# A graph and recurrent kernel: edge places computed in six parts beside the scatter, and four unread TensorE products in every recurrent step

## The reference, cut to what matters

```python
x_proj = jnp.einsum('btd,gd->btg', x, W_ih) + b_ih + b_hh
def step(carry, xp):
    h, c = carry
    gates = xp + h @ W_hh.T                      # 256 -> 1024
    i, f, g, o = jnp.split(gates, 4, axis=-1)
    c = jax.nn.sigmoid(f) * c + jax.nn.sigmoid(i) * jnp.tanh(g)
    h = jax.nn.sigmoid(o) * jnp.tanh(c)
    return ((h, c), h)
```

## Time and profile before

| | us |
|---|---|
| three executions | 31170.26, 31184.28, 31179.84; median 31179.84 |
| profiled execution, its own time | 31181.4 |
| its span, first to last instruction | 31179.7 |
| PE busy | 26082.7 (84% of the span) |
| PE weight loads | 21913.3 (70%) |
| DVE busy | 11210.6 (36%) |
| ACT busy | 8537.5 (27%) |
| POOL busy | 7747.7 (25%) |
| mean granted TensorE clock | 0.631 of full |

### The profile page before, as it was taken

One profiled execution on the slowest core, in us unless ns is written; L12 is line 12 of the kernel. 1 busy time (PEld: TensorE's weight loads), 2 busy tenths in 40 slices (PEclk: granted clock), 3 DMA queues, 4 the chain that ended last, 5 costly groups with the idle time before them and its releaser, 6 DMA issues. The chain is left out here.

```text
span 31179.7 us, 1124934 instructions
## 1 busy us (share of the span) xinstructions
PE 26082.7 (84%) x456492; PEld 21913.3 (70%) x456597; DVE 11210.6 (36%) x40897; ACT 8537.5 (27%) x40793; POOL 7747.7 (25%) x12838
## 2 busy tenths in 40 slices
PE   0002556788777799999999999999999999999998
PEld 0002334333665688888888888888888888888887
DVE  7002333777555333333333333333333333333334
ACT  0000001688111132222222222232222222222322
POOL 1776771677776000000000000000000000000000
PEclk9998778999888655555555555555555555555555
DMA  0002331000333000000000000000000000000000
GB/s 36 1 1 71 104 105 24 7 2 2 97 99 93 33 1 1 1 1 1 1 1 1 1 1 1 1 1 1 1 1 1 1 1 1 1 1 1 1 1 9
DMA packets 370440, 557.74 MB, mean 18 GB/s; under 512 B 177610, under 2 KB 254830, under 8 KB 369006
## 3 DMA queue, kind: packets, MB, share of 16 engines
q0 software_dynamic: 263728, 458.62, 5.9%
q1 hardware_dynamic: 106686, 98.81, 1.0%
HBM read 496.64 MB, written 60.32 MB: 18 GB/s over the span
## 5 line engine op out<-in xcount | busy, mean ns | idle before, releaser
L1160 PE MATMUL banks<-ls_xp,ls_sel 128*128 128x64 f32 x37500 | 9641.6, 430 | 18.2 <-DVE ls_w L1223 18.2
L1160 PEld LDWEIGHTS banks<-ls_xp,ls_sel 128*128 128x128 f32 x37500 | 8466.7, 325 | 1376.1 <-issue 1376.1
L1173 PE MATMUL banks<-ls_w,ls_ht 128*2 128x64 f32 x200000 | 6735.4, 311 | 0.0
L1147 POOL TENSOR_TENSOR ls_d<-ls_tf,ls_cell 128x2 f32<-128x2 f32 x6250 | 1241.9, 199 | 19305.7 <-ACT ls_tf L1188 19305.7
L1173 PEld LDWEIGHTS banks<-ls_w,ls_ht 128*2 128x2 f32 x200000 | 5585.4, 127 | 0.0
L1229 DVE STREAM_TRANSPOSE ls_f_cols<-banks 128x64 f32<-128x64 f32 x6250 | 1561.5, 250 | 7590.1 <-PE banks L1167 7590.1
L1178 PE MATMUL banks<-ls_w,ls_ht 128*2 128x64 f32 x100000 | 4068.7, 311 | 0.0
L436 PE MATMUL banks<-ag_rows,ag_pick 128*128 128x256 f32 x3328 | 1204.8, 526 | 3392.9 <-DMA ag_rows<-y_table,ag_idx 3359.0
L1167 PE MATMUL banks<-ls_w,ls_ht 128*1 128x64 f32 x100000 | 3777.1, 299 | 0.0
L1188 ACT ACTIVATE ls_tf<-ls_f_cols 128x2 f32<-128x2 f32 x6250 | 1286.8, 206 | 8783.7 <-DVE ls_f_cols L1229 8776.7
L436 PEld LDWEIGHTS banks<-ag_rows,ag_pick 128*128 128x128 f32 x3328 | 831.5, 262 | 3765.6 <-DMA ag_rows<-y_table,ag_idx 2759.9
(11 more groups left out here) (256 smaller groups left out, 19365.3 us busy)
## 6 DMA issues: line engine op xcount, KB each, us to landing
ag_rows<-y_table,ag_idx POOLq DMA_INDIRECT x1664, 2.7
mx_rows<-alpha_dst_table,mx_idx POOLq DMA_INDIRECT x1664, 2.3
at_rows<-wh_table,at_idx POOLq DMA_INDIRECT x1664, 2.8
projections<-xp_out SPq DMA_DIRECT2D x7, 3584.0 KB, 10.4
rec_table<-st_rec,st_idx POOLq DMA_INDIRECT x1563, 2.1
ls_xp<-projections SPq DMA_DIRECT2D x1250, 20.0 KB
rec_table<-zero POOLq DMA_DIRECT2D x5, 2496.0 KB, 20.9
rec_part<-rec_table SPq DMA_DIRECT2D x5, 2496.0 KB, 19.9
```

The lines of the kernel that those rows point to most:

```text
L1160: x = nc.tensor.matmul(bank[:, 0:HD], sel[:, u, :], xp[:, b, lo:lo + HD], start=True, stop=False)
L1173: m = nc.tensor.matmul(banks_ig[s][32 * j:32 * j + 2, 0:HD], ht[:, v, c, 1 - r:3 - r], w[:, c, j, lo:lo + HD], start=False, stop=(r, c) == ...
```

## The change: what it does, and the diff

`stage_normalise` keeps only its constants, and `stage_places` becomes empty except for the number of parts, 6. All that they did stands in `stage_scatter`, in one block of the program, so that the engines are no longer held by a barrier between them. DVE counts all edges as before; it makes `REC` after the count and not ahead of it. Then it gives places in six parts of 260 columns (the last has 263), each with its own loop over the 49 blocks. One more small copy per block carries the running offset from part to part. ACT begins to stage records as soon as part 0 has its places (`placed`), and POOL's indirect DMAs follow. Behind part 5 DVE makes `BW` in a loop of its own, and then the layer norm of x, whose square root is one instruction for all blocks, which ACT does after part 3's records. x is loaded and y stored by SP in the same block. POOL clears the record tables before its first indirect DMA, as before.

```diff
+            for c in range(PARTS):
+                act.wait_ge(placed, c + 1)
+                if c == 0:
+                    stage_half(0, 0)
+                    stage_half(0, 1)
+                with act.Fori(0, IT - (c == 0)) as t:
+                    restage(t, c * IT + (c == 0))
+                if c == ROOT_AT:
+                    act.wait_ge(normed, 2 * NB + 1)
+                    nc.scalar.sqrt(root[:, :], ve[:, :]).then_inc(rooted, 1)
...
+            def place(c, a, w):
+                base = c * NB * 4
+                with dve.Fori(0, NB) as b:
+                    vec.tensor_single_scalar(in_b[:, 0:w], hi[:, a:a + w], item[:, ds(b, 1)], ALU.is_equal).then_inc(s_item, 1)
+                    dve.wait_ge(s_item, b * 4 + (base + 1))
+                    vec.tensor_tensor_scan(rank[:, 0:w], in_b[:, 0:w], in_b[:, 0:w], off[:, ds(b, 1)], ALU.add, ALU.bypass).then_inc(s_item, 1)
+                    dve.wait_ge(s_item, b * 4 + (base + 2))
+                    own_wait(dve, g)
+                    vec.tensor_copy(off[:, ds(b, 1)], rank[:, w - 1:w]).then_inc(s_item, 1)
+                    vec.copy_predicated(pos[:, 0:w], in_b[:, 0:w], rank[:, 0:w]).then_inc(s_item, 1)
+                    dve.wait_ge(s_item, b * 4 + (base + 4))
...
+            for c in range(PARTS):
+                place(c, c * W, W if c < PARTS - 1 else W + REST)
```

```diff
+    wake = sb("ls_wake", [P, 512], BF16)
...
                     if u == LU - 1:
                         x.then_inc(xp_used, 1)
+                    for j in range(4):
+                        nc.tensor.matmul(g["ps"][6][32 * j:32 * j + 1, :], wake[:, 0:1], wake[:, :], start=True, stop=True, tile_position=(0, 32 * j))
                     pe.wait_ge(h_ready, i * PER + (k + 1))
...
-                    nc.gpsimd.tensor_tensor(d1[:, 2:2 * SC:SC], tf[:, :], c_now, ALU.mult).then_inc(f_mul, 1)
+                    nc.gpsimd.tensor_tensor(d1[:, 2:2 * SC:SC], tf[:, :], c_now, ALU.mult).then_inc(scan_in, 1)
...
+            vec.memset(wake[:, :], 1.0)
...
-                    dve.wait_ge(f_mul, i * PER + (k + 1))
-                    dve.wait_ge(ig_act, i * PER + (k + 1))
+                    dve.wait_ge(scan_in, i * (2 * PER) + (2 * k + 2))
```

More of the change, by code:

```diff
@@ L136, in stage_normalise @@
 def stage_normalise(nc, sb, sem, g):
-    t = norm_tiles(sb, sem, "ln0")
-    yt = sb("ln0_out", [P, GB, D])
-    x_loaded, pads, step, stored, made = sem("x_loaded"), g["started"], t["step"], sem("y_stored"), sem("consts_made")
+    made = sem("consts_made")
     with nc.Block() as block:
[L141 to L149, removed]
         @block.gpsimd
@@ L159, in _, with stage_scatter @@
             pool.wait_ge(made, 3)
[L161 to L174, removed]
-def stage_places(nc, sb, sem, g):
[L179 to L189, removed]
+def stage_places(nc, sb, sem, g):
+    g["parts"] = 6
+def stage_scatter(nc, sb, sem, g):
+    SH = SU // 2
+    per = SU // WAYS
+    FULL = EC // SU
+    REST = EC - FULL * SU
+    PARTS = g["parts"]
+    IT = FULL // PARTS
+    W = IT * SU
+    ROOT_AT = 3
+    src = sb("src_i", [P, EC], I32)
+    hi_i = sb("hi_i", [P, EC], I32)
+    hi = sb("hi", [P, EC])
+    dst = sb("dst_i", [P, EC], I32)
+    ew = sb("ew_in", [P, EC])
+    in_all = sb("in_all", [P, EC])
+    in_b = sb("in_b", [P, W + REST], I32)
+    rank = sb("rank", [P, W + REST])
+    pos = sb("pos", [P, W + REST])
+    pos_i = sb("pos_i", [P, W + REST], I32)
+    col_i = sb("col_i", [P, W + REST], I32)
     upper = sb("upper", [P, P])
     ones = sb("ones_c", [P, P])
-    cnt = sb("cnt", [EP, NB])
+    cnt = sb("cnt", [P, NB])
     tot = sb("tot", [P, NB])
@@ L339, in _, with stage_half, restage @@
                 pool.wait_ge(g["scattered"][k], 16 * (1 + FULL * per + (k < REST)))
+        @block.tensor
+        def _(pe):
+            pe.wait_ge(ready, 4)
+            pe.wait_ge(counted, NB)
+            nc.tensor.matmul(counts_ps[:, 0:NB], upper[:, :], cnt[:, :], start=True, stop=True)
+            nc.tensor.matmul(g["ps"][1][:, 0:NB], ones[:, :], cnt[:, :], start=True, stop=True).then_inc(summed, 1)
+        @block.scalar
+        def _(act):
+            def stage_half(i, h):
+                nc.scalar.copy(recs[:, h, :, :], g["REC"][:, ds(i * SU + h * SH, SH), :]).then_inc(staged, 1)
+                nc.scalar.copy(idx[:, h, :], g["POS"][:, ds(i * SU + h * SH, SH)]).then_inc(staged, 1)
+            def restage(t, it):
+                for h in range(2):
+                    for k in range(WAYS):
+                        act.wait_ge(g["scattered"][k], t * (16 * per) + (it - 1) * (16 * per) + 16 * (1 + (h + 1) * per // 2))
+                    stage_half(t + it, h)
+            for c in range(PARTS):
[8 more added lines that the diff above has]
+                    nc.scalar.sqrt(root[:, :], ve[:, :]).then_inc(rooted, 1)
+            for k in range(WAYS):
+                act.wait_ge(g["scattered"][k], (FULL - 1) * (16 * per) + 16 * (1 + per // 2))
+            nc.scalar.copy(recs[:, 0, 0:REST, :], g["REC"][:, FULL * SU:EC, :]).then_inc(staged, 1)
+            nc.scalar.copy(idx[:, 0, 0:REST], g["POS"][:, FULL * SU:EC]).then_inc(staged, 1)
```

201 lines of the change are left out of this document (104 added, 97 removed).

## The result

The changed kernel takes 23909.92 us (median of four executions, 23903.88 to 23914.42) against 31180.4 us for the kernel before (31170.26 to 31184.28): a ratio of 0.7669, 95% interval 0.7655 to 0.7682. The forecast of 24227 us was 317 us too long, and the time lies in its range. Of the 7270 us gained, the recurrent stage brings nearly all.

The account below looks back on a forecast made before the run. PE at half clock was taken to bound the recurrent stage, 3.287 us a step. From 31181.4 us, less 6542 for the stage and 412 for the front, came 24227 us, range 23350 to 28300.

Parts of the forecast that it names:

- The clock: Recurrent stage: four unread 512-column products a step raise PE's granted clock from 0.50 to 1.00, and it stays.
- Rivals 1 and 3: Recurrent stage: clock stays at half, 33440 us, chance 0.09; or rises and falls again, 28800 us, chance 0.06.
- rival 3: Recurrent stage: clock rises and falls again, half the steps at 2.24, half at 3.71 us; 28800 us, chance 0.06.
- The step at full clock: Recurrent step: chain from h to h sums to 2.16 us, mean 2.24 with the turn; stage 14000 us, gain 6542.
- hand-over to PE: Recurrent step: from h ready on DVE to PE's start on the h products, 0.12 us.
- f and i,g products: Recurrent step on PE: 48 records in 12 groups of 0.056 us, the last landing 0.84 us after the first starts.
- i,g landed to the scan: Recurrent step: transpose, tanh and hand-overs shrink from 0.66 to 0.59 us as o products land sooner.
- one wait less: DVE before the scan: priced at nothing, at most some hundredths of a microsecond a step.
- rival 2: PE in the recurrent step: instruction issue limits h products, 28290 us, or the four run in turn, 27300; chance 0.14.
- The turn: Recurrent loop, once in ten steps: ACT's table load is exposed, costing about 0.8 us, 0.08 a step.
- The front: Stages up to the scatter: first indirect DMA at about 248 in place of 672 us; gain 412 us (380 to 430).
- the cost of DVE beside POOL: Scatter: DVE's work beside POOL's indirect DMAs slows them by 0 to 27 us, taken as 10.

Follow-up runs that it names:

- the first four kernels: Changed kernel without the unread products (25065 to 31975 us), with the old front (25232), with 80 unread products once (25099), with one full-width product (25058).

## Why the prediction was right

**The clock** was the main step, and it held: 1.00 from some 5 us into the stage to its end. The reason given was in part right. The stage does lack something that raises the clock, and unread products supply it (it came up in all 30 executions of the ten kernels that have them in front of or in the changed stage, and in four of the seven executions without them). But the text took 0.50 as the fixed state of the stage without them, lacking long streams in every step, and it is not: both the old and the new stage have two states, and in the changed steps a short push at the start does as much as 25000 products. What decides the state was not found. Rivals 1 and 3 did not come about in the changed kernel; rival 3 is what eight products or a body of 50 steps bring, by a cause it did not name, the loading of code, as the instruction packets tell.

**The step at full clock.** The terms, as predicted and as measured in the step above: hand-over to PE 0.12, measured 0.06 (15001.82 to 15001.88); f and i,g products 0.84, measured 0.85; i,g landed to the scan 0.59, measured 0.59 (15002.73 to 15003.32); scan to h 0.61, and 0.61 from 15003.32 to the next h. The sum 2.16, measured 2.112. The first is the term that was mis-sized: it was read in the attention, behind a DVE instruction of 1.24 us, where the step has one of 0.16. Whether the length makes the difference was not tested. The error of the sum is 0.048 x 5625 = 270 us in the ordinary steps and (2.96 - 2.853) x 625 = 67 in the turns, 337 in all. The 0.59 hides a second error: **one wait less** was priced at nothing, as its inputs are there by then, and it is worth 0.066 us a step, 374 us in all. Without it the third term would have been 0.65.

**PE's issue** did not limit it (rival 2): the 16 records of f start 0.22 us before those of i and g, 0.014 us a record, where the rival had 0.027. The 32 records of i and g take 0.63 us and those of f 0.40 at full clock, against 1.08 and 0.60 at half, and these lengths hold the fixed latency of the last record.

**The turn** was put at 0.8 us and measured 0.74, by the chain that was named: table load, tanh of f, POOL, scan.

**The front** started at 248.5 where 248 was worked out, so its terms are right in sum; the place loop's turn is 2.30 us where 2.25 was. The other parts, beside POOL's DMAs, take 125 us each in place of 110, and are hidden as was said; in the three disturbed traces of the first four kernels they took 272 to 379 and were not. The term that failed is the cost of DVE beside POOL: 10 us, with 27 as its bound, taken from stages with other DVE work. It is 54, and nearly all of it in the 49 instructions of L340, whose form had no row beside an indirect DMA. Gain 369 in place of 412.

In sum: stage 338 us better than forecast (6880 against 6542), front 43 worse, and 31 from the middle stages and -2 from the finish that were not in the sum: 324 us by the spans. By the medians it is 317.

What the change is worth apart from the clock can be told too. The kernel before once ran at full clock by itself: 24844 us, 924 more than the changed kernel run beside it (23921). It has no trace, but its profiled execution with 80 products ahead of the loop has one, 24758 us, 854 more than the profiled execution of the kernel after. This can be divided: front 369, middle stages 36, recurrent stage 451 (first h to last h, 14110.9 against 13659.6), finish -1. Of the 451 the second wait is 374, and turns that are 0.094 us longer (2.947 against 2.853) are 59, which leaves 18. Why that one execution without a push took 86 us more is open.

## What to carry over

A stage on TensorE that the profile shows always busy at a granted clock of 0.50 may have a second, faster state that it keeps once it is in it. A few long products right ahead of its loop are the cheap test, in several executions, since the clock comes up in some without them and can be lost again with them. Where a chain of short instructions bounds the step, count the waits and not only what they wait for, and see what the last instruction of a loop body holds up on ACT. Before instructions are added to a long loop body, look at the `instruction` rows of the DMA queues: where they show thousands of packets, the body is loaded again and again.

## What was not expected of the hardware

- A stage of 20 ms stays at 1.2 GHz with PE recorded as busy throughout, and the same code stays at 2.4 GHz with PE busy for 87% of the time; which of the two an execution takes varies (three and four of seven).
- PE's loop body has a size from which code is fetched in the loop. With ten steps of 74 product records each (462488 / 6250) there are 12 instruction packets on queue q8 in the whole run. With four more in each step there are 1326, and pauses of 9.64 - 2.24 = 7.4 us in nearly every fourth turn.
- One more wait before the scan, on a semaphore that is already there, costs this step 0.066 us.
- A DVE instruction of 128x1664 with two long inputs (L340) doubles the time for which POOL is held by an indirect DMA (2.05 against 0.96 us); a scan and a predicated copy of 260 columns leave it unchanged.
- In three traces with the new front DVE's place loops stood idle on issue beside POOL's indirect DMAs, for 527 us before the first instruction of the loop alone in one of them, and the front's gain of 369 us fell to about 100.
